# A decoder of two layers on one core: the next pass's key projections at other places of the order, coupled steps in halves, and added products without a result

## The reference

```python
x = layernorm(x + attn0(x))                # 16 heads of 64, softmax, output matrix
x = layernorm(x + xattn0(x, ctx))          # 16 heads of 16 over 120 context tokens
x = layernorm(x + bitffn(x))               # quantized gate, up, down
x = layernorm(x + gated_attn(x))           # decays in place of scores, then an MLP
x = layernorm(x + xattn1(x, ctx, ctx))     # softmax over QUERIES, 2 key sets, 2 inner norms
x = layernorm(x + coupled(x))
def coupled(x):                            # the two last stages are where the change is
    gf = global_net(mean of x over tokens)
    out = x
    for _ in range(3):
        tf = sigmoid(gelu(gelu(gelu(out @ w1 + b1) @ w2 + b2) @ w3 + b3) @ w4 + b4)
        out = out + (0.1 + range * (0.7 * gf + 0.3 * tf - 0.5) * 2) * twist(out)
```

## Time and profile before

| | |
|---|---|
| median of 3 runs | 1265.72 us (1265.17 to 1266.19) |
| profiled execution, its own time | 1278.1 us |
| span of the profiled execution | 1275.9 us |
| mean granted TensorE clock | 0.922 |
| pass starts of cross1 (first L512 of the stage) | 277.21, 578.09, 868.33, 1157.86 us |
| TensorE busy | 84% |

### The profile page before, as it was taken

The page is one execution under the profiler, slowest core; times in us unless marked ns, Lnnn a source line. Parts: engine busy times, 40 slices in busy tenths (PEclk is TensorE's granted clock), DMA queues, the critical chain, the costliest instruction groups (busy, mean ns, idle before and its releaser), DMA issues.

```text
span 1275.9 us, 19390 instructions
## 1 busy us (share of the span) xinstructions
PE 1075.6 (84%) x7058; PEld 692.6 (54%) x7058; DVE 765.4 (60%) x1834; ACT 649.0 (51%) x1744; POOL 331.1 (26%) x670
## 2 busy tenths in 40 slices
PE   5987988899879998899788998899778987788874
PEld 2454645674545654585454655585454664475452
DVE  0177476556647558565847657664856747864655
ACT  1465345247347744546647734554637724544622
POOL 1056301231115520222025530221124630131012
PEclk9988999897689999999989999998899998998676
DMA  9302200000000000000000000000000000000000
GB/s 238 132 2 90 62 1 9 1 0 2 1 1 18 18 17 1 8 1 1 1 1 18 18 17 2 8 1 1 1 1 1 18 1 2 1 1 1 1 1 17
DMA packets 30446, 22.76 MB, mean 18 GB/s; under 512 B 16656, under 2 KB 29456, under 8 KB 30224
## 3 DMA queue, kind: packets, MB, share of 16 engines
q1 hardware_dynamic: 29760, 19.93, 5.7%
q10 hardware_dynamic: 592, 1.59, 0.3%
HBM read 19.42 MB, written 2.10 MB: 17 GB/s over the span
## 4 chain that ended last, share of the span: by engine, by line
PE 59%; DVE 18%; ACT 11%; issue 5%; POOL 4%; DMA 1%; SPq 0%; POOLq 0%; DVEq 0%; ACTq 0%
PE PS L542 8%; PE PS L529 4%; PE PS L690 4%; PE PS L929 4%; ACT work L1445 4%; PE PS L589 3%; POOL work L2149 3%; PE PS L778 3%; PE PS L572 3%; PE PS L659 2%; PE PS L942 2%; PE PS L676 2%; PE PS L903 2%; PE PS L977 2%; PE PS L641 2%
## 5 line engine op out<-in xcount | busy, mean ns | idle before, releaser
L2123 POOL TENSOR_TENSOR rstd<-var,minus_half 128x2 f32<-128x2 f32 x64 | 45.8, 715 | 464.1 <-DVE var L1569 464.1
L1445 ACT ACTIVATE work<-PS,nmax 120x256 f32<-120x256 f32 x256 | 117.7, 489 | 44.8 <-DVE nmax L1984 44.5
L2149 POOL TENSOR_SCALAR work<-work,inv 128x256 f32<-128x256 f32 x256 | 125.3, 507 | 0.0
L1984 DVE TENSOR_REDUCE nmax<-PS 120x2 f32<-120x512 f32 x128 | 82.0, 685 | 71.0 <-PE PS L929 70.8
L1628 DVE TENSOR_REDUCE nmax<-PS 128x2 f32<-128x512 f32 x128 | 82.2, 684 | 67.3 <-PE PS L641 67.2
L1261 ACT ACTIVATE work<-PS,nmax 128x256 f32<-128x256 f32 x256 | 118.1, 482 | 4.1 <-DVE nmax L1628 4.0
L2118 POOL TENSOR_TENSOR pool_pause<-minus_half 128x1 f32<-128x1 f32 x96 | 30.1, 314 | 263.1 <-DVE inv L1635 138.7
L929 PE MATMUL PS<-x_room 32*120 32x256 f32 x512 | 72.7, 462 | 14.9 <-ACT work L1445 11.2
L676 PE MATMUL PS<-work 128*64 128x256 f32 x512 | 71.2, 400 | 9.6 <-DVE work L1639 9.5
L641 PE MATMUL PS<-work 64*128 64x256 f32 x512 | 72.7, 400 | 1.9 <-ACT work L1261 1.9
L929 PEld LDWEIGHTS PS<-x_room 32*120 32x120 f32 x512 | 44.5, 207 | 41.9 <-issue 33.1
(11 more groups left out here) (278 smaller groups left out, 2441.3 us busy)
## 6 DMA issues: line engine op xcount, KB each, us to landing
turned_x<-in_xT_dram SPq DMA_DIRECT2D x8, 256.0 KB, 3.1
xa<-in_x_dram SPq DMA_DIRECT2D x4, 512.0 KB, 4.5
out_dram<-x_room SPq DMA_DIRECT2D x4, 512.0 KB, 3.0
rows<-in_rows_dram ACTq DMA_DIRECT2D x1, 1536.0 KB, 8.3
late<-in_L_attn_W_dram SPq DMA_DIRECT2D x2, 768.0 KB, 8.0
wv<-in_L_attn_kernel_dram SPq DMA_DIRECT2D x2, 512.0 KB, 11.3
wq<-in_L_attn_kernel_dram SPq DMA_DIRECT2D x2, 512.0 KB, 7.8
wk<-in_L_attn_kernel_dram SPq DMA_DIRECT2D x2, 512.0 KB, 7.5
```

Of the source, the lines that this page charges most:

```text
L1445: op = act.activation(e1[:, par, r, kv, :], bank(SCORE_1[r])[0:M, kv * S:(kv + 1) * S], ACT.Exp, bias=nmax1[:, par, r, kv:kv + 1], accum_o ...
L1984: dve.tensor_reduce(nmax1[:, par, r, :], bank(SCORE_1[r])[0:M, :].rearrange("p (v s) -> p v s", v=2), AX.X, ALU.max, negate=True).then_inc ...
L2149: op = pool.tensor_scalar(e0[:, u % 2, st, hh, :], e0[:, u % 2, st, hh, :], inv0[:, u % 2, hh, st:st + 1], 1.0, ALU.mult, ALU.mult)
```

## The change

- Key blocks move. Blocks 0, 1 and 2 leave the score loop: 0 stands at its end, before the last `weigh_1`, and 1 and 2 behind the last `out_1`. Block 3 is split, one half behind each of the two turns of c0. Block 4 goes before the third step of the coupled cycles, block 5 into the fourth step behind `scores0(then, 0)`, block 6 behind `scores0(it, 1)`, block 7 behind `scores0(it, 2)`. Each block is now made in two halves of 256 columns, one for each sequence. ScalarE's copies, the banks (`KEY_FILL`) and the waits follow; `scores0` waits for its own block only.
- `couple` works on halves of 256 columns, each with its own semaphore count, and so do `gelu_1` and the two products of `net_2`. The operations that prepare later cycles are put into `cross_over`, which comes behind all `couple` calls of the step.
- `idle_products(count)` multiplies weights of bf16 by themselves (512 columns) into bank 7, where nobody reads them: 2 each at n = 12, 16 and 28 of the score loop and 3 in the third coupled step of every pass; in the last pass, in place of key blocks, 7 at the end of the loop, 12 behind `out_1`, 7 before the third step and 8 in the fourth.
- In the score loop, VectorE's `stats_z0`, `centre_z0` and `scale_z0` come one, two and three n later.

```diff
-KEY_FILL = (7, 7, 7, 7, 5, 7, 5, 7)
+KEY_FILL = (7, 5, 7, 7, 7, 5, 7, 7)
...
+    def idle_products(count):
+
+        for _ in range(count):
+            pe.matmul(bank(7), wg16[:, 0, 0:P], wg16[:, 0, 0:512], start=True, stop=True)
...
-    def keys0(it, j):
-
-        if j == 0:
-            pe.wait_ge(q0_kept.sem, q0_kept.at(it, J))
-        elif j == 4:
-            pe.wait_ge(p1_done.sem, p1_done.at(it - 1, GX * HC))
-        elif j == 6:
-            pe.wait_ge(gg3_tanh.sem, gg3_tanh.at(it - 1, NB))
-        elif j == 7:
-            pe.wait_ge(summed["out"].sem, summed["out"].at(it - 1, 1))
-        else:
-            pe.wait_ge(k0_kept.sem, k0_kept.at(it, min(j, 4)))
+    def keys0(it, j, b):
+
+        if b == 0:
+            if j == 0:
+                pe.wait_ge(q0_kept.sem, q0_kept.at(it, J))
+            elif j == 1:
+                pe.wait_ge(p1_done.sem, p1_done.at(it - 1, GX * HC))
+            elif j == 5:
+                pe.wait_ge(gg3_tanh.sem, gg3_tanh.at(it - 1, NB))
+            elif j == 6:
+                pe.wait_ge(coef_kept.sem, coef_kept.at(it - 1, 1))
+            else:
+                pe.wait_ge(k0_kept.sem, k0_kept.at(it, j - 1 if j == 2 else j))
         for k in range(KD):
-            mm = pe.matmul(bank(KEY_FILL[j]), wk0[:, k, j * P:(j + 1) * P], turned_x[:, k, :],
-                           start=(k == 0), stop=(k == KD - 1))
-        mm.then_inc(k0_done.sem, 1)
+            mm = pe.matmul(bank(KEY_FILL[j])[:, b * S:(b + 1) * S], wk0[:, k, j * P:(j + 1) * P],
+                           turned_x[:, k, b * S:(b + 1) * S], start=(k == 0), stop=(k == KD - 1))
+        if b == NB - 1:
+            mm.then_inc(k0_done.sem, 1)
+
+    def both_keys0(it, j):
+        for b in range(NB):
+            keys0(it, j, b)
     def project_first():
...
             if last is not None:
                 pe.wait_ge(tf_tanh.sem, tf_tanh.at(last, CB - 1))
         else:
             pe.wait_ge(p0_done.sem, p0_done.at(it, 2 * (u - 1)))
-        if u == NB * (J - 2):
-            pe.wait_ge(k0_kept.sem, k0_kept.at(it, J))
+        if b == 0:
+            pe.wait_ge(k0_kept.sem, k0_kept.at(it, j + 1))
         for st in range(TS):
             for hh in range(2):
...
     def net_2(it, r, b):
-        pe.wait_ge(hh1_kept.sem, hh1_kept.at(it, NB * r + b + 1))
         for k in range(KD):
+            pe.wait_ge(hh1_kept.sem, hh1_kept.at(it, KD * (NB * r + b) + k + 1))
...
                     turn(it, "c0", xs["5"], b)
+                    if then is not None:
+                        keys0(then, 3, b)
                     net_1(it, b)
                     global_net_1(it, b, then)
                     net_1_twisted(it, b)
+            if step == STEPS[2]:
+                if then is not None:
+                    both_keys0(then, 4)
+                else:
+                    idle_products(7)
             if step == STEPS[-1] and then is not None:
                 pe.wait_ge(z_freed.sem, z_freed.at(it, NB))
                 scores0(then, 0)
+                both_keys0(then, 5)
+            if step == STEPS[-1] and then is None:
+                idle_products(8)
             for b, r in step:
+                if step == STEPS[2] and r == 2:
+                    if then is not None:
+                        pe.wait_ge(k0_kept.sem, k0_kept.at(then, 5))
+                    idle_products(3)
                 net_2(it, r, b)
                 if r == 0:
...
         for u in range(U0 + 2):
-            if last is not None and u == 0:
-                keys0(it, J - 2)
             if u + 1 < U0:
                 scores0(it, u + 1, last)
             if last is not None and u == 0:
-                keys0(it, J - 1)
+                both_keys0(it, J - 2)
                 turn_final(last, 1)
+            if last is not None and u == 1:
+                both_keys0(it, J - 1)
             if u == U0 - 1:
                 out0(it, 0, 0, 3)
...
             scores_1(it, n)
+            if n > 10 and n % HP == 0 and n not in (20, 24):
+                if then is not None and n == 12:
+                    pe.wait_ge(q0_kept.sem, q0_kept.at(then, J))
+                idle_products(2)
             if n == 2:
                 turn_normed(it, "x4", xs["4"], 1)
                 if then is not None:
                     queries0(then, 7)
             if n == 6:
                 queries_1(it, 1)
-            if then is not None and n in (6, 10, 14):
-                keys0(then, (n - 6) // 4)
             if n % HP == 2 and n > HP:
                 weigh_1(it, n // HP - 1)
             if n == GX // 2 * HC + 4:
                 turn_back(it, 0)
             if n == GX // 2 * HC + 8:
                 out_1(it, 0)
+        if then is not None:
+            both_keys0(then, 0)
+        else:
+            idle_products(7)
         weigh_1(it, 2 * GX - 1)
         turn_back(it, 1)
         out_1(it, 1)
         if then is not None:
-            for j in (3, 4, 5):
-                keys0(then, j)
+            both_keys0(then, 1)
+            both_keys0(then, 2)
+        else:
+            idle_products(12)
     def one_pass(it, last=None, then=None):
...
                 op = act.activation(e1[:, par, r, kv, :], bank(SCORE_1[r])[0:M, kv * S:(kv + 1) * S], ACT.Exp,
                                     bias=nmax1[:, par, r, kv:kv + 1], accum_out=sum1[:, par, r, kv:kv + 1])
             op.then_inc(p1_done.sem, 1)
-            if then is not None and n in (7, 11, 15):
-                keep_k0(then, (n - 7) // 4)
+        if then is not None:
+            keep_k0(then, 0)
         load_table(ACT.Gelu)
         if then is not None:
-            keep_k0(then, 3)
-        if then is not None:
-            keep_k0(then, 4)
-            keep_k0(then, 5)
+            keep_k0(then, 1)
+            keep_k0(then, 2)
     def coupled_ffn(it, then=None):
...
             for c in range(KD):
+                if r == 0:
+                    act.wait_ge(hh1_done.sem, hh1_done.at(it, b + 1))
+                else:
+                    act.wait_ge(z_ready.sem, z_ready.at(it, KD * (NB * (r - 1) + b) + c + 1))
                 src = bank(HIDDEN[b])[:, c * S:(c + 1) * S] if r == 0 else z_now[:, b, c, :]
-                op = act.activation(h1[:, c, b * S:(b + 1) * S], src, ACT.Gelu,
-                                    bias=col["L1_ffn_cn_b1"][:, c:c + 1])
-            op.then_inc(hh1_kept.sem, 1)
+                act.activation(h1[:, c, b * S:(b + 1) * S], src, ACT.Gelu, bias=col["L1_ffn_cn_b1"][:, c:c + 1]
+                               ).then_inc(hh1_kept.sem, 1)
...
                     keep_c0(b)
+                    if then is not None and b == NB - 1:
+                        keep_k0(then, 3)
                 gelu_1(r, b)
+                if then is not None and (b, r) == STEPS[2][0]:
+                    keep_k0(then, 4)
+                if then is not None and (b, r) == STEPS[3][0]:
+                    keep_k0(then, 5)
                 if r == 0:
                     global_1(b)
...
                 scale_values(m - 1)
             if r == 3 and par == 0 and m > 1:
                 keep_o1(m // 2 - 1)
-            if n == GX // 2 * HC + 5:
+            if n == GX // 2 * HC + 6:
                 stats_z0(0)
+            if n == GX // 2 * HC + 7:
                 centre_z0(0)
-            if n == GX // 2 * HC + 7:
+            if n == GX // 2 * HC + 10:
                 scale_z0(0)
         sum_z1(0)
         scale_values(2 * GX - 1)
         dve.tensor_scalar(cpl[r][:, b, :], tf[:, b, :], reach3[:, 0:1], base[:, b:b + 1], ALU.mult, ALU.add
                           ).then_inc(cpl_done.sem, 1)
         dve.wait_ge(cpl_done.sem, cpl_done.at(it, n))
-        by = cpl[r][:, b, :].unsqueeze(1).to_broadcast([P, KD, S])
-        if r == 0:
-            plain, crossed = (bank(m[b]).rearrange("p (c s) -> p c s", c=KD) for m in (HIDDEN, TWISTED))
-            dve.wait_ge(hh1x_done.sem, hh1x_done.at(it, b + 1))
-            dve.tensor_tensor(z_part[:, b, :, :], crossed, by, ALU.mult).then_inc(z_scaled.sem, 1)
-            dve.wait_ge(z_scaled.sem, z_scaled.at(it, (1, 3)[b]))
-            dve.tensor_tensor(z_now[:, b, :, :], plain, z_part[:, b, :, :], ALU.add).then_inc(z_ready.sem, 1)
-            dve.wait_ge(z_ready.sem, z_ready.at(it, n))
-            dve.tensor_tensor(z_part[:, b, :, :], plain, by, ALU.mult).then_inc(z_scaled.sem, 1)
-            dve.wait_ge(z_scaled.sem, z_scaled.at(it, (2, 4)[b]))
-            dve.tensor_tensor(z_twisted[:, b, :, :], crossed, z_part[:, b, :, :], ALU.subtract).then_inc(z_freed.sem, 1)
-        else:
-            dve.wait_ge(z_freed.sem, z_freed.at(it, b + 1))
-            dve.tensor_tensor(z_part[:, b, :, :], z_twisted[:, b, :, :], by, ALU.mult).then_inc(z_scaled.sem, 1)
-            dve.wait_ge(z_scaled.sem, z_scaled.at(it, (5, 6)[b]))
-            dve.tensor_tensor(z_now[:, b, :, :], z_now[:, b, :, :], z_part[:, b, :, :], ALU.add).then_inc(z_ready.sem, 1)
+        by = cpl[r][:, b, :]
+        for c in range(KD):
```

(23 more changed lines are left out.)

19 lines of the change are left out of this document (7 added, 12 removed).

## The result

The kernel after took 1212.28 us (median of 1237.07, 1213.06, 1210.52 and 1211.51), the kernel before 1265.45 beside it. The ratio is 0.956, with a 95% interval of 0.952 to 0.961: faster. The gain is about 54 us where 34.5 were forecast, and 1212 is the very edge of the range. In what follows a loop is said to fall when TensorE's granted clock drops from 2.4 to 1.2 GHz in it for some 25 us or more.

What follows compares the result with a forecast made beforehand. TensorE's order and clock were taken to bound the kernel. Structure of 22.5 us (11.4 + 1.6 + 2.3 + 7.2) and 12 for the clock made 34.5, from 1265.7 to 1231 us; range 1212 to 1255.

Steps and rivals of the forecast that it cites:

- Clock, 12 us: TensorE's clock in and behind the score loops: 22 of 47 us come back, less 10 dropped, leaving 12.
- ceiling: Most clock time that could come back: 18 us in the score loops and 29 behind them, 47 together.
- The 10 dropped: Cut from the clock gain because the timed executions seem to lack about 10 us of slow time to begin with.
- all clock comes back: Rival: all 47 us of clock time return beside the 22.5 of structure; 1212 to 1222, say 1218 us; chance 0.20.
- Key blocks, 11.4: Score loop: taking key blocks out starts exponentials earlier, 3.8 us in each of three passes.
- Spread norm operations, 1.6: Score loop: VectorE's later norm operations delay one maximum less, 0.4 us in each pass.
- Turn of c0, 2.3: Behind the output product: with two blocks left, the turn waits for the norm, 0.76 us gained in each of three passes.
- Coupled steps, 7.2: Halves and later cross_over shorten steps 3 and 4 by 1.8 us in each of four passes (bounds 2 and 10).
- Step 4, 0.4: Fourth coupled step: halves gain 0.9 us less 0.5 for longer operations, 0.4 a pass (bounds -0.6 and 0.8).
- Only cover: Rival: blocks only change cover, the loop gains nothing and the clock stays as it was; 1256 us; chance 0.07.
- Every loop falls: Rival: a few idle products are too little, so every score loop falls to half clock; 1253 us; chance 0.19.
- slower: Rival: clock stays down through the output product, blocks end behind the norm, coupled steps gain nothing; 1274 us; chance 0.07.

Runs made afterwards that it cites:

- x2: Kernel before with idle products alone, in the waits that the change fills; no block moved, no halves: 1232.5 us, ratio 0.970.
- x13: Kernel after unchanged, run again in six executions: 1226.0 us, ratio 0.966.
- x7: Kernel after with key blocks 0 to 2 back in the score loop and idle products in their places at the loop's end: 1225.5 us, ratio 0.965.
- x6: Kernel after with two more pairs of idle products in the score loop, at n = 4 and n = 8: 1214.3 us, ratio 0.956.
- x9: Kernel after with couple, gelu_1 and net_2 in full width and old order, plus idle pairs at n = 4 and 8: 1219.1 us, ratio 0.959.
- x10: Kernel after with full-width coupled steps in the new order, plus idle pairs at n = 4 and 8: 1212.7 us, ratio 0.955.
- x4: Kernel before with the key blocks moved as in the change and nothing else: 1266.2 us, ratio 0.996.
- x1: Kernel after with every idle product left out, blocks and halves as changed: 1238.4 us, ratio 0.973.
- x5: Kernel before with the coupled steps' halves and new order alone: 1287.3 us, ratio 1.012.
- x3: Kernel after with couple, gelu_1 and net_2 as before, in full width and old order: 1234.4 us, ratio 0.973.
- x8: Kernel after with full-width coupled steps but the new order kept: 1223.4 us, ratio 0.963.
- x12: Kernel after with idle products in the score loop and at its end alone: 1243.9 us, ratio 0.972.
- x14: Kernel after with full width, new order, idle pairs at n = 4 and 8, idle products at last pass's c0 turns; six executions: 1212.1 us, ratio 0.957.

## Why the prediction was off

The direction held; two terms of the sum were far out, in opposite directions.

- **Clock, 12 us: the step that failed.** The ceiling was 47 us, of which I took 22 "as some loop will fall", and then dropped 10 because the median seemed to lack that time to begin with. It was the first cut that was wrong. x2 moves nothing, and its eight windows last 401.9 us against 446.7 of the kernel before, cut alike: 44.8 us come back, 19.4 in the loops (ceiling 18) and 25.4 behind them (ceiling 29), though three of the four loops stay a little under full clock (0.93 to 0.96). The ceiling was sound, and "some loop will fall" had no price that came out of rows. It did come true in the recorded execution of the kernel after and in x13 (1226 us, one loop at 55), at 8 to 15 us a loop.
- **The 10 dropped** were sound in kind. The sums start from an execution of 1278.1 us, and time that an execution at the median did not lose can't be won back from it: x2 gains 44.8 us in the windows against that execution and 37.5 by medians, where the medians of the chip start 8.1 us lower. But the rival "all clock comes back" counted it twice. 1278.1 - 22.5 - 47 = 1208.6 is where such a kernel ends, wherever one starts from; the 10 us added to reach 1218 had no ground. This rival's mechanism came nearest, but that its figure did is partly luck, as the 10 us offset a structure put 9 us too high. That 1212 is the lower edge of the range comes from this error: by its own terms the rival stood 3 us below it.
- **Key blocks, 11.4: 9.9.** 3.30 a pass (x7 against x6) for 3.8. The pass 4 that served as check had half-clock time of its own.
- **Spread norm operations, 1.6: 0** (46.88 against 46.91).
- **Turn of c0, 2.3: 0 at full clock.** The 0.76 us were counted as structure, but the blocks of the earlier trace rows started 1.15 us late behind transposes and an output product at half clock, and the norm only 0.46. With the clock back they meet within 0.2 us in the old order (x2).
- **Coupled steps, 7.2: 3.7.** 51.69 to 50.82 is 0.87 in three passes (the order -1.44, the halves +0.31, the moved blocks +0.26, which the prediction put at 0), and x9's 59.62 to x13's 58.56 about 1.1 in the last. "If halves of additions take over 0.6 us" was named as what would break it: they take 0.83 in step 3. The Trainium skill, VectorE: DVE Perf Modes, section on the errata of SBUF sources, would make it 0.42; the trace does not agree where GpSimd works at the same time (629.34 above, 0.89 us). In pass 2 no addition of these operands stands without such company. My price for halves took the rows of single operations without such company; the earlier trace rows had the warning, a full addition of 1.09 us.
- **Structure together, 22.5: 13.6.** It was put 9 us too high and hid part of the clock's error: by luck the miss was 19 us and not 28.
- **Outside the windows, 0: some 5.** The recorded executions of the kernel before and of x6 (1278.1 and 1214.7 us) differ by 63.4, of which 58.4 lie in the windows. For the other 5 there was no term. The sum redone, 58.4 and 5 less the 10, is 53, where 54 was measured.
- **Step 4, 0.4 of the above: 0.** From the fourth tanh to the sixth the kernel after takes 7.44 us in pass 2, x10 and x9 7.41, the kernel before 7.41: the additions of the halves again last 0.83 us each, and eat what the earlier start of the gelu gives. Block 5, named as what might bind here, ends at 638.5, before the second half of the gelu (638.75 to 639.26) that net_2 needs.
- **Rivals.** "Only cover" is out by x7. "Every loop falls" and "slower" did not come; x4 and the recorded execution of x1 show the first at work when no idle products stand there, with three and with four fallen loops. The second is not shown: x5 was longer, but in its record not by a late output product and turn.

The Trainium skill's rule from TensorE: Matmul & The Clock Gate, section "Why this matters for your kernels", is that idle gaps between bursts of products bring the clock down. It names longer gaps than any in x13's fallen loop, and the trace does not agree with it as it stands: the longest wait there is 1.33 us, the clock fell in it, and did not in pass 2 in an equal wait. Nor does the rule say why the clock stayed down while TensorE was busy for 27.34 of 27.68 us, mostly with narrow products. These runs do not separate the wait from the narrow products around it.

**What stays open.** Why one loop falls and an equal one holds. x13's passes 2 and 3 run the same instructions with the same times up to the fall, so what decides lies outside the loop or is chance, and the losses of x3, x5, x8 and x12 against their neighbours can't be laid to their edits. Whether a change in the coupled steps bears on a loop 185 us later was not traced. How blocks and halves without idle products (x1) gain 28 us more than blocks alone (x4) is open too, since x1's record is of an execution 27 us above its median. The windows leave 829 us outside them before, 830 in x2 and 821 to 828 in the other kernels. 2 to 4 us of that lie in pass 1 ahead of cross1, where no edit is; 0.3 us each in the stretches behind passes 1 and 2 (185.5 to 185.2 in most); the stretch in front of pass 4 takes 177 to 182 us in the various kernels, at clocks of 0.93 to 0.98, and was not split. How often loops of the kernel after fall, and whether the chip matters, is known from ten executions only.

**A better version.** x14 (full width, new order, pairs at n = 4 and 8, products at c0's turn of the last pass) ran at 1212.1 us where the kernel after ran at 1226.0 on the same chip, with intervals of the ratio that overlap by 0.001. One of its six executions, at 1216.4, lies above the 1206 to 1213 expected of all. Its lead is mostly the loop that does not fall: 11.4 us of the 13 between the two recorded executions.

## What to carry to other kernels

Price an edit twice, once with all rows at full clock and once with the clock that it leaves behind, and use only rows of one clock in one difference: a wait read from a stretch with half-clock products beside it may vanish when these do. When a sum starts from one execution and the answer is a median, subtract their difference once. Wide products without a result, put into TensorE's waits, cost nothing at full clock in the loops here and were worth 37 us, so try them before moving work; then count executions, since one median hides whether a loop falls in some of them. And put the addition that the next engine waits for first before cutting it in halves.

## What the runs showed of the hardware

- A score loop with equal instructions took 43.59 us in one pass and 55.03 in the next of the same execution (x13), by the clock alone. The clock fell in a wait of 1.33 us that the other pass had too, and was down for 27 us with TensorE 99% busy (27.34 of 27.68).
- Idle products of bf16, 512 columns, two at a time: four more of them left the loop at 43.58 us.
- An addition of two operands of 256 columns took 0.83 us on VectorE with GpSimd at work, against 0.42 for those of that width that read one operand from a PSUM bank with GpSimd at rest (that one of the earlier trace rows, and 627.65 in pass 2 of the kernel after); the full width took 1.10. The two causes are not separated, but a multiplication of two operands from SBUF took 0.42 where GpSimd had just begun (629.22) and 0.61 where it worked throughout (630.43).
- Halves in the coupled steps alone left the whole kernel 1.2% longer (x5) at a lower mean granted clock, 0.909 where the kernel before had 0.931 (both by the execution at the median).
- Blocks and halves in the waits brought the clock behind the loops of passes 1 to 3 to 1.00 without any idle product (x1).
